# A float32 layer with 64 routed experts on one core: the sums of signs split over two stages, the last wait moved to SyncE, and the up weights held until earlier additions have landed

## The reference

```
xn = layernorm(x)                                    # 8192 tokens x 512
attn = rfs(xn) @ rfs(weights).T                      # 512 random features
scores = sigmoid(xn @ router_w)                      # 64 experts in 8 groups
# the best 4 groups by their best expert, then the best 8 experts;
# weights divided by their sum, times 2.5
# each expert takes its first 256 tokens (CAP = 256)
expert_out[e] = (silu(d[e] @ gate_w[e]) * (d[e] @ up_w[e])) @ down_w[e]
moe = zeros.at[token].add(expert_out[e][slot] * weight)
shared = (silu(xn @ sg) * (xn @ su)) @ sd
out = x + attn + moe + shared
```

## Time and profile before

| what | us |
|---|---|
| three runs, median | 1300.33 |
| lowest and highest | 1300.19, 1310.35 |
| the profiled execution's own time | 1298.49 |
| its span in the trace | 1296.8 |
| granted clock, mean | 0.995 |
| PE busy | 1276.2 (98%) |
| DVE, ACT, POOL busy | 928.8, 657.0, 431.0 |

### The profile page before, as it was taken

One profiled execution on the slowest core, in us unless ns is written; L12 is line 12 of the kernel. 1 busy time (PEld: TensorE's weight loads), 2 busy tenths in 40 slices (PEclk: granted clock), 3 DMA queues, 4 the chain that ended last, 5 costly groups with the idle time before them and its releaser, 6 DMA issues.

```text
span 1296.8 us, 23014 instructions
## 1 busy us (share of the span) xinstructions
PE 1276.2 (98%) x7585; PEld 1119.1 (86%) x7585; DVE 928.8 (72%) x1853; ACT 657.0 (51%) x1126; POOL 431.0 (33%) x344
## 2 busy tenths in 40 slices
PE   8999999999999999999999999999999999999995
PEld 7888888888888888888889999999999999999994
DVE  7887787867878678785655777767766767776762
ACT  6422223222232222322255777777777777777773
POOL 2000000000000000000014667777676656676663
PEclk9999999999999999999999999999999999999998
DMA  8246554565545655445447999999999999999995
GB/s 311 82 137 169 127 134 103 141 168 133 122 105 143 168 127 125 107 112 136 136 132 218 291 276 302 276 312 287 294 287 291 295 294 282 291 296 288 296 258 79
DMA packets 202778, 263.66 MB, mean 203 GB/s; under 512 B 49269, under 2 KB 137209, under 8 KB 202745
## 3 DMA queue, kind: packets, MB, share of 16 engines
q1 hardware_dynamic: 173272, 191.40, 50.1%
q0 software_dynamic: 28672, 71.32, 24.9%
q10 hardware_dynamic: 800, 0.53, 0.1%
HBM read 178.18 MB, written 71.39 MB: 192 GB/s over the span
## 4 chain that ended last, share of the span: by engine, by line
PE 53%; DMA 32%; POOL 10%; issue 3%; DVE 0%; ACT 0%; POOLq 0%
DMA out_dram<-outs,slot_cols 16%; POOL out_dram L1728 10%; PE pmm L1331 9%; PE pmm L1332 9%; PE pmm L1333 9%; DMA out_dram<-feat,slot_cols 8%; DMA out_dram<-xbuf,slot_cols 8%; PE pout L1331 7%; PE pout L1333 7%; PE pout L1332 7%; PE plp L1396 2%; POOL xbuf L1718 1%; PE plp L1405 1%; PE ptr L1343 0%; PE pout L1518 0%
## 5 line engine op out<-in xcount | busy, mean ns | idle before, releaser
L1332 PE MATMUL pmm<-xt_lo,proj_hi 128*128 128x256 f32 (+1 forms) x776 | 244.3, 315 | 0.0
L1333 PE MATMUL pmm<-xt_hi,proj_lo 128*128 128x256 f32 (+1 forms) x776 | 244.3, 315 | 0.0
L1332 PE MATMUL pmm<-xt_lo,sgu_hi 128*128 128x256 f32 (+1 forms) x764 | 240.3, 315 | 0.0
L1333 PE MATMUL pmm<-xt_hi,sgu_lo 128*128 128x256 f32 (+1 forms) x764 | 240.2, 314 | 0.0
L1331 PE MATMUL pmm<-xt_hi,proj_hi 128*128 128x256 f32 (+1 forms) x744 | 235.8, 317 | 0.6 <-DVE xt_lo L845 0.6
L1331 PE MATMUL pmm<-xt_hi,sgu_hi 128*128 128x256 f32 (+1 forms) x732 | 231.6, 316 | 0.0
L1712 POOL TENSOR_TENSOR earlier<-earlier,chosen 128x64 bf16<-128x64 bf16 x64 | 24.3, 379 | 610.4 <-DVE chosen L966 606.6
L1718 POOL DMA_INDIRECT xbuf<-rows,slot_cols x128 | 171.8, 1342 | 88.4 <-issue 33.9
L564 ACT ACTIVATE feat<-pmm,ab 128x512 f32<-128x512 f32 x66 | 45.4, 687 | 286.5 <-PE pmm L1333 286.5
L1332 PEld LDWEIGHTS pmm<-xt_lo,proj_hi 128*128 128x128 f32 x776 | 145.7, 188 | 11.4
L1333 PEld LDWEIGHTS pmm<-xt_hi,proj_lo 128*128 128x128 f32 x776 | 145.7, 188 | 10.3
(11 more groups left out here) (214 smaller groups left out, 2648.4 us busy)
## 6 DMA issues: line engine op xcount, KB each, us to landing
raw<-in_L_ffn_gate_w_dram SPq DMA_DIRECT2D x64, 512.0 KB, 6.4
raw<-in_L_ffn_up_w_dram SPq DMA_DIRECT2D x64, 512.0 KB, 6.4
raw<-in_L_ffn_down_w_dram SPq DMA_DIRECT2D x64, 512.0 KB, 5.5
outs<-in_L_attn_x_dram SPq DMA_DIRECT2D x32, 512.0 KB, 4.0
out_dram<-outs SPq DMA_DIRECT2D x32, 512.0 KB, 3.1
xbuf<-in_L_attn_x_dram SPq DMA_DIRECT2D x52, 256.0 KB, 7.5
raw<-xn SPq DMA_DIRECT2D x52, 256.0 KB, 6.2
rows<-raw SPq DMA_DIRECT2D x39, 256.0 KB, 4.2
```

Of the source, the lines that this page charges most:

```text
L1332: pe.matmul(psum, lh, rl, start=False, stop=False)
L1333: ins = pe.matmul(psum, ll, rh, start=False, stop=final and n == len(pairs) - 1)
```

## The change

Four things. (1) `sum_signs` takes `parts`; its first four activations stand at the end of stage k = 1, the other four at the end of k = 2, and stage k = 2 rounds both weight halves in the usual place. (2) DVE's `slot_tokens` stands at the start of stage k = 3 and no longer at the end of k = 2 (`pass_blocks` stays at the end of k = 0). (3) SP loads the up half of n only when `added` has reached 32 (n-4), that is, when the additions of experts 0 to n-5 have landed; the first pass of SP's loop is peeled off, since that count is not positive there for all n. (4) The final wait for `added` stands at the end of SP's program and no longer at the end of POOL's.

```diff
--- before.py
+++ after.py
@@ -530,6 +530,8 @@
                 for m, source in enumerate((gate_w, up_w)):
                     sp.wait_ge(egu_hi_made[m], e.n - 1)
                     sp.wait_ge(egu_lo_made[m], e.n - 1)
+                    if m == 1:
+                        at_least(sp, added, 16 * CB * (e.n - 4))
                     load_half(e.b, m, source[e.n])
 
             def refill_down(e):
@@ -540,17 +542,22 @@
 
             refill_gate_up(turn(3))
             refill_down(turn(2))
-            with sp.Fori(0, CHUNKS - 3) as m:
+            def refill_four(m):
                 for k in range(CHUNK):
                     e = Turn(2 * m + 2 + k // 2, k % 2, k // 2)
                     refill_gate_up(e)
                     refill_down(e.prev())
                     if k == 1:
                         load_chunk(m + 3)
+
+            refill_four(0)
+            with sp.Fori(1, CHUNKS - 3) as m:
+                refill_four(m)
             for n in range(E - 2 * CHUNK, E):
                 refill_gate_up(turn(n))
                 refill_down(turn(n - 1))
             refill_down(turn(E - 1))
+            sp.wait_ge(added, 16 * CB * E)
 
 
         @block.scalar
@@ -598,9 +605,9 @@
                 at = slice(2 * half, 2 * half + 2)
                 act.activation(xt_hi[g.b][:, at, :], xt_whole[:, at, :], copy).then_inc(xt_hi_made, 1)
 
-            def sum_signs(n):
-
-                for q in range(2):
+            def sum_signs(n, parts=(0, 1)):
+
+                for q in parts:
                     act.wait_ge(lookup_done, 2 * n + q + 1)
                     for e in range(2):
                         for c in range(CB):
@@ -766,16 +773,13 @@
                     act.activation(e_outs[e.q][c], pout[c], copy, scale=slot_w[e.q][:, c:c + 1]).then_inc(
                         e_out_made, 1)
 
-            def stage(e, next_rows=True, next_weights=True, out_prev=True, look=None, first=False,
-                      looked=False):
+            def stage(e, next_rows=True, next_weights=True, out_prev=True, look=None, first=False):
                 e_silu(e)
                 if next_weights:
-                    gate_up_hi(e.next(), (0,) if looked else (0, 1))
+                    gate_up_hi(e.next())
                 if next_rows:
                     e_turned_hi(e.next())
                 e_hidden_hi(e)
-                if looked:
-                    gate_up_hi(e.next(), (1,))
                 if first:
                     for b in range(2):
                         act.wait_ge(out_stored[b], 16 * GROUPS)
@@ -786,14 +790,14 @@
                 if next_rows:
                     down_hi(e)
                 if look is not None:
-                    sum_signs(look)
+                    sum_signs(look[0], (look[1],))
 
             e_turned_hi(turn(0))
             stage(turn(0), next_weights=False, out_prev=False)
             stage(turn(1), first=True)
             def chunk(m):
                 for k in range(CHUNK):
-                    stage(four(2 * m + 1, k), look=m + 2 if k == 1 else None, looked=k == 2)
+                    stage(four(2 * m + 1, k), look=(m + 2, k - 1) if 1 <= k <= 2 else None)
 
             chunk(0)
             with act.Fori(1, CHUNKS - 2) as m:
@@ -1287,7 +1291,9 @@
                                   hid_hi[:, e.b].rearrange("p a b -> p (a b)").bitcast(F32),
                                   ALU.subtract).then_inc(e_hid_lo_made, 1)
 
-            def stage(e, next_rows=True, next_weights=True, look=None):
+            def stage(e, next_rows=True, next_weights=True, blocks=None, tokens=None):
+                if tokens is not None:
+                    slot_tokens(tokens)
                 if next_weights:
                     gate_up_lo(e.next(), (0,))
                 e_hidden(e)
@@ -1297,8 +1303,8 @@
                     gate_up_lo(e.next(), (1,))
                 e_hidden_lo(e)
                 down_lo(e)
-                if look is not None:
-                    look[0](look[1])
+                if blocks is not None:
+                    pass_blocks(blocks)
 
             e_turned_lo(turn(0))
             output(turn(GROUPS - 1), 3)
@@ -1307,8 +1313,7 @@
             stage(turn(1))
             with dve.Fori(0, CHUNKS - 2) as m:
                 for k in range(CHUNK):
-                    stage(four(2 * m + 1, k), look=(pass_blocks, None, slot_tokens, None)[k] and (
-                        (pass_blocks, None, slot_tokens, None)[k], m + 2))
+                    stage(four(2 * m + 1, k), blocks=m + 2 if k == 0 else None, tokens=m + 2 if k == 3 else None)
             for n in range(E - 6, E - 2):
                 stage(turn(n))
             e_turned_lo(turn(E - 1))
@@ -1746,7 +1751,6 @@
                     add_rows(turn(n - 4))
             for n in range(E - 4, E):
                 add_rows(turn(n))
-            pool.wait_ge(added, 16 * CB * E)
 
 
 # ---- launch: one core; inputs and outputs as the reference has them ----
```

## The result

| | before | after |
|---|---|---|
| median, us | 1301.17 (4 runs) | 1353.78 (4 runs, 1351.99 to 1355.29) |
| profiled execution, us | 1298.49 | 1353.84 |
| span, us | 1296.8 | 1352.0 |
| ratio of the runs | | 1.0397, 95% interval 1.0363 to 1.0432 |

The four runs of the kernel before in this comparison gave 1300.2 to 1310.4 us. The change makes the kernel 4% slower. The forecast was 1294.7 us and the range ended at 1304: wrong in sign and size. The rival that came true is A, which had 0.12 and 1320.7 us.

What follows compares the result with a forecast made beforehand. PE was taken to set the pace, with additions running behind at the same pace. Span 1296.8 - 2.5 - 3.1 = 1291.2, plus 1.7 for execution and 1.8 to the median, gave 1294.7 us; 8-in-10 range 1290 to 1304.

Steps and rivals of the forecast that it cites:

- rival A: DMA engines between two landings: additions too slow, so late up loads slow PE; 0.5 us an interval, 1320.7 us, chance 0.12.
- part 3: SP's wait before the up load: loads then start together at a landing; taken as 0, bytes per interval unchanged.
- Bounds by landings: Landing times of additions used to bound the wait's effect: smallest 4.8, median 6.8, largest 8.3 us; the median was taken.
- Two things are full there: Expert part: PE busy 49.97 of 50 us and DMA share 1.04, both read as full.
- the descriptor phase: Time after a landing when POOL makes descriptors: loads would now fill it, an argument against rival A.
- The margin: Up half's arrival ahead of ACT's need under the new wait: 2.5 us, 0.5 at worst.
- Part 1: ACT's sums of signs in two stages: PE gains 0.18 us in each of 14 places, 2.5 us.
- cost nothing: Dropping the order `looked` in stage k = 2 and moving DVE's `slot_tokens` to k = 3: no effect on time.
- The additions follow PE, so PE's 2.5 us reach the end: Step in the sum: the 2.5 us PE saves in the expert stages shorten the whole span.
- Rival D: Expert part: loads change nothing and PE's gain is lost as additions don't follow PE; 1297.2 us, counted within the forecast's 0.58.
- Part 2: Final wait moved to SP: POOL's 3.01 us drain runs under the flight of the data, gain 3.1 us.
- rival B: End of the kernel: POOL's drain waits for the data, so part 2 is worth 0; 1297.8 us, chance 0.17.

Runs made afterwards that it cites:

- half_up_free: The changed kernel without the wait before the up load and with up loads of 256 KB instead of 512: 1292.7 us (one run).
- bunch_free: The changed kernel without the wait for additions; gate, up and the previous expert's down load start together once a stage: median 1317.8 us, ratio to before 1.0008.
- signs_only: The kernel before with only the split sums, moved slot_tokens and plain order of rounding: median 1312.6 us, ratio to before 1.0069.
- no_hold: The changed kernel without the wait before the up load: median 1298.1 us, ratio to before 0.9974.
- tie_start: The changed kernel, but the up load of n waits for POOL's signal that additions of n-5 are issued, not landed: median 1293.0 us, ratio 0.9936.
- end_only: The kernel before with only the final wait moved from POOL to SP: median 1299.6 us, ratio to before 0.9983.
- hold_only: The kernel before with only the wait before the up load added: median 1352.0 us, ratio to before 1.0391.
- loose_hold: The changed kernel with the up load of n waiting for additions of n-6 instead of n-5: median 1299.4 us (1293.5 to 1340.6).

## Why the prediction was wrong, point by point

**The step that failed** is in part 3: "I take 0, since the bytes in each interval stay the same and the median row is one with just these bytes in it". The bytes did stay the same, 2727 KB, and the interval went from 9.34 to 10.33 us all the same. I priced the traffic by volume and not by when it flows. I had written that the loads now "start together at a landing, just when POOL makes descriptors and no additions move", and booked it as a gain. It is the reverse: a load issued at the landing moves nothing yet, and the loads that used to be under way there are done. The 0.8 us of DMA share missing behind each landing are most of the 1.0 us; where the rest goes is open. Bounds by landings (4.8, 6.8, 8.3) were wide enough for it; the value between them was not, and the range did not follow the bounds as it should have.

**Reading the kernel before.** "Two things are full there" was half right. half_up_free shows that full engines were not what made the additions follow each other without a gap: with 27 GB/s less they still do. What the additions do have is a limit close to PE's pace, and by the table a phase that costs them a few tenths puts them over it. ("The last 18 slices" of nine tenths are 17, a slip without weight.) That closeness I had seen and used for rival A alone.

**Rival A** had the place, the deciding point (an interval above 9.3) and the sign. Its price, 0.5 us an interval and 26 us above the forecast, was half or less of what came: 1.0 us, and 59 us (53 above before). Its mechanism, the burst, is not sufficient by bunch_free; the Trainium skill's rule of turns between queues ("DMA: Bandwidth & Descriptors", section "Queues, rings and completion order"), which I cited for it, moved no term, and no run here tells it apart. Its chance of 0.12 was too low: against it stood only the sentence on the bytes and the one on the descriptor phase, and both were the step that failed.

**The margin** of 2.5 us at a landing of 6.4 was right in size and mattered little. The additions fell back by a microsecond an expert and used up what there was: PE's stages are 9.13 to 9.6 us from expert 2 to 14, and from 16 to 59 they are 9.3 to 11.7, 10.3 in the mean.

**Part 1** had the right mechanism and the wrong size, and then the gain did not arrive. In the changed kernel's early stages, which the additions don't hold yet, the same three stages as in the earlier trace rows (1204.70 to 1232.41, 27.71 us) take 27.40:

```profile
756.11 0.31 PE L1592 MATMUL pmm<-xt_hi,proj_hi 128*128 128x320 f32 x1
...
765.25 0.31 PE L1592 MATMUL pmm<-xt_hi,sgu_hi 128*128 128x320 f32 x1
...
774.38 0.31 PE L1592 MATMUL pmm<-xt_hi,proj_hi 128*128 128x320 f32 x1
...
783.51 0.31 PE L1592 MATMUL pmm<-xt_hi,sgu_hi 128*128 128x320 f32 x1
```

So 0.31 a chunk and not 0.18, and 14 x 0.31 = 4.3 us. The stage from 56 to 57 gains 0.18, as I had it (9.32 to 9.14). The one behind it, 9.25 in the earlier trace rows, gains another 0.12 (9.13), and I had put that one at nothing ("cost nothing" for the order `looked` and for `slot_tokens`); which of the two held it up, no run separates.

"The additions follow PE, so PE's 2.5 us reach the end" was no safe step either. In signs_only PE keeps stages of 9.25 us in the mean and stands still nowhere until expert 38, while the additions fall from 3.0 us behind their first output at expert 4 to 13.1 at expert 40; in no_hold they go from 4.6 to 10.7. Rival D said that the gain would be lost, not that it could turn into a loss. Only with tie_start does it come through in every run: 1293.0 is close to what I had forecast for parts 1 and 2.

**Part 2** was worth 1.5 us and not 3.1. The rows of the changed kernel that answer to the earlier trace rows:

```profile
L95 POOLq DRAIN  x1: 8769/8769/8769, 1343.0 to 1343.0; - x1
L95 SPq COMPARE_BRANCH  x1: 38/38/38, 1350.2 to 1350.2; - x1
...
L95 SPq EVENT_SEMAPHORE  x1: 17/17/17, 1352.0 to 1352.0; - x1
```

POOL's drain began at 1343.0, beside the last additions, and lasted 8.77 us, to 1351.8: 1.6 us beyond SP's wake at 1350.2. So it is neither the forecast (a work of 3 us of its own, done in parallel) nor rival B (worth nothing): it ends behind the data, and then after half the time that it took before. end_only measures it in the time: 1299.6 against 1300.9, ratio 0.9983, with an interval that just reaches 1. The Trainium skill's 12 ns ("VectorE: DVE Perf Modes", section "The DRAIN you can't avoid") do not hold here: POOL's drain took 3.0 us before and 8.8 after, and the measurement decides.

## What to carry to other kernels

When a transfer is tied to the landing of another one, ask what is in flight at that instant: if every other load has landed by then, the DMA engines are short of work until the next one flows, once in each turn (here 0.8 us of 10.3), and the bytes don't show it. Where two chains run at nearly the same pace (here 9.3 us both), test a tie at several release points before judging it; released when the additions were issued rather than when they had landed, the same tie was worth 60 us (1353.8 against 1293.0). And where two such chains run, look at the scatter of the runs, not at one of them.

## What the runs showed of the hardware

A drain of POOL at the program's end, issued while POOL's own DMAs are in flight, ended 1.5 to 1.6 us after SP saw their landing, in all 14 profiles in which SP has the final wait; it ended 5.1 to 5.4 us after POOL's last instruction. That it waits for the data is the likelier reading, since it keeps closer to the landing; but the landings themselves differ by only 0.35 us there, so it is not proven. Where POOL has waited for the landing itself (before, hold_only, signs_only), the drain still takes 3.0 us from there. The rows of tie_start, 1281.6 to 1290.7 with SP awake at 1289.1:

```profile
L95 POOLq DRAIN  x1: 9099/9099/9099, 1281.6 to 1281.6; - x1
L95 SPq COMPARE_BRANCH  x1: 38/38/38, 1289.1 to 1289.1; - x1
...
L95 SPq EVENT_SEMAPHORE  x1: 17/17/17, 1290.9 to 1290.9; - x1
```

Additions into DRAM behind one another take up to a microsecond longer an interval at unchanged bytes, by when other transfers start (9.28 us in tie_start, 10.33 with the change). A DMA share of 1.00 to 1.04 does not say that the engines are at their limit: half_up_free has 1.00 at 265 GB/s, tie_start 1.04 at 293, with the same 9.28 us between additions. And one program with two chains this close gave 1293.5 and 1340.6 us (loose_hold), at mean granted clocks of 0.996 and 0.994.
